# Transposing attention probabilities in 32x32 squares on VectorE and moving the squares by DMA and ScalarE, in place of TensorE transposes

## What is computed

```python
# x: (8, 1024, 384) float32, adj: (8, 1024, 1024) bool, six heads of 64 features
q = _heads(seq_inputs @ Wq + bq)
k = _heads(seq_inputs @ Wk + bk)
v = _heads(seq_inputs @ Wv + bv)
scores = jnp.einsum('bhqd,bhkd->bhqk', q, k) / np.sqrt(HEAD_SIZE)
bias = jnp.where(graph_mask, 0.0, NEG)[:, None]
probs = jax.nn.softmax(scores + bias, axis=-1)
ctx = jnp.einsum('bhqk,bhkd->bhqd', probs, v)
ctx = ctx.transpose(0, 2, 1, 3).reshape(seq_inputs.shape[0], seq_inputs.shape[1], H)
return ctx @ Wf + bf
# and around it
x = _layernorm(x + _L0_gnn_ref(x, ...), axis=-1)
```

## Time and profile before

| | before |
|---|---|
| time, median of three runs | 1510.48 us (1510.31 to 1511.2) |
| profiled execution, its time | 1509.4 us |
| its span | 1507.4 us |
| granted TensorE clock over the span | 0.997 of full speed |
| TensorE matmuls busy | 1471.1 us, 98% |
| VectorE busy | 898.2 us, 60% |
| ScalarE busy | 873.4 us, 58% |
| GpSimd busy | 378.2 us, 25% |
| DMA engines, share of their time on the kernel's own queue | 10.5% |

### The profile page before, as it was taken

The page is one execution under the profiler, slowest core; times in us unless marked ns, Lnnn a source line. Parts: engine busy times, 40 slices in busy tenths (PEclk is TensorE's granted clock), DMA queues, the critical chain, the costliest instruction groups (busy, mean ns, idle before and its releaser), DMA issues.

```text
span 1507.4 us, 32054 instructions
## 1 busy us (share of the span) xinstructions
PE 1471.1 (98%) x11088; PEld 1141.7 (76%) x11088; DVE 898.2 (60%) x1769; ACT 873.4 (58%) x1637; POOL 378.2 (25%) x676
## 2 busy tenths in 40 slices
PE   7999999999999999999999999999999999999996
PEld 6777787777877778777787777877778777787764
DVE  5666645665556655666555665566655666465654
ACT  4566626666266662666636665366654666546662
POOL 2112242122411224122141221412214122141222
PEclk9999999999999999999999999999999999999998
DMA  3110101100011000100001100011001110000000
GB/s 129 36 40 30 29 27 38 38 29 29 27 50 29 29 29 24 50 30 29 30 24 50 40 29 20 29 49 35 29 19 37 50 29 30 15 25 19 30 22 28
DMA packets 47925, 51.41 MB, mean 34 GB/s; under 512 B 9089, under 2 KB 47745, under 8 KB 47745
## 3 DMA queue, kind: packets, MB, share of 16 engines
q1 hardware_dynamic: 47744, 49.12, 10.5%
HBM read 36.31 MB, written 12.78 MB: 33 GB/s over the span
## 4 chain that ended last, share of the span: by engine, by line
PE 92%; DVE 3%; issue 2%; ACT 1%; POOL 1%; DMA 0%; DVEq 0%; SPq 0%; ACTq 0%; POOLq 0%
PE turn_ps L457 23%; PE context_ps L470 22%; PE score_ps L444 20%; PE misc_ps L356 4%; PE misc_ps L355 4%; PE misc_ps L354 4%; PE score_ps L354 3%; PE score_ps L355 3%; PE score_ps L356 3%; DVE prob L660 1%; PE context_ps L354 1%; PE turn_ps L354 1%; PE context_ps L356 1%; PE context_ps L355 1%; PE misc_ps L362 1%
## 5 line engine op out<-in xcount | busy, mean ns | idle before, releaser
L660 DVE CUSTOM_DVE_ANT_0 prob<-score_ps,mask 128x1024 f32<-128x1024 f32 x384 | 455.0, 1222 | 252.5 <-PE score_ps L444 232.7
L568 ACT ACTIVATE prob_t<-turn_ps 128x512 f32<-128x512 f32 x384 | 229.5, 598 | 431.6 <-PE turn_ps L457 431.6
L559 ACT ACTIVATE prob<-prob,row_min 128x1024 f32<-128x1024 f32 x384 | 442.1, 1151 | 64.3 <-DVE row_min L660 64.3
L457 PE MATMUL turn_ps<-ident,prob 128*128 128x128 f32 x3072 | 413.1, 276 | 9.8 <-ACT prob_t L568 5.5
L457 PEld LDWEIGHTS turn_ps<-ident,prob 128*128 128x128 f32 x3072 | 337.7, 140 | 94.8 <-issue 78.0
L470 PE MATMUL context_ps<-prob_t,v_all 128*64 128x256 f32 x3072 | 372.1, 385 | 0.8 <-ACT prob_t L568 0.8
L470 PEld LDWEIGHTS context_ps<-prob_t,v_all 128*64 128x64 f32 x3072 | 204.6, 136 | 148.9 <-issue 64.0
L806 POOL TENSOR_TENSOR context_lo<-context,context_hi 128x256 fp32r<-128x256 f32 x96 | 70.6, 735 | 938.6 <-ACT context_hi L582 938.6
L669 DVE COPY prob_t<-turn_ps 128x512 f32<-128x512 f32 x192 | 131.7, 686 | 30.7 <-PE turn_ps L457 30.2
L444 PE MATMUL score_ps<-k_hi,q_hi 64*128 64x512 f32 x768 | 140.9, 444 | 4.8 <-issue 3.8
L444 PE MATMUL score_ps<-k_lo,q_hi 64*128 64x512 f32 x768 | 120.4, 390 | 0.0
(11 more groups left out here) (85 smaller groups left out, 1834.9 us busy)
## 6 DMA issues: line engine op xcount, KB each, us to landing
x_in<-in_x_dram SPq DMA_DIRECT2D x32, 384.0 KB, 3.4
inv_rows<-spread_dram SPq DMA_DIRECT2D x192, 64.0 KB, 2.6
out_dram<-res SPq DMA_DIRECT2D x32, 384.0 KB, 2.5
adj_in<-in_adj_dram SPq DMA_DIRECT2D x64, 128.0 KB, 2.2
spread_dram<-inv_turned SPq DMA_DIRECT2D x384, 0.5 KB
prob_t<-in_L_gnn_Wk_dram SPq DMA_DIRECT2D x1, 576.0 KB, 4.3
prob_t<-in_L_gnn_Wq_dram SPq DMA_DIRECT2D x1, 576.0 KB, 7.1
prob_t<-in_L_gnn_Wv_dram SPq DMA_DIRECT2D x1, 576.0 KB, 8.3
```

The source lines that it names most:

```text
L457: last = pe.transpose(turn_ps[:, half, i, :], prob[:, u % 4, kt * P:(kt + 1) * P], ident[:])
L559: nc.scalar.activation(prob[:, t % 4, :], prob[:, t % 4, :], ACT.Exp, scale=-1.0, bias=row_min[:, t % 4:t % 4 + 1], accum_out=row_sum[:, t ...
L568: nc.scalar.activation(prob_t[:, pair % 2, head, 0:4, qt * P:(qt + 1) * P], turn_ps[:, 0], ACT.Copy).then_inc(copied[0], 1)
L660: nc.vector.tensor_tensor_reduce(prob[:, t % 4, :], score_ps[:, t % 2, :], mask[:, qt, :], 1.0, HUGE, ALU.add, ALU.min, row_min[:, t % 4:t ...
```

## The change

The change writes the kernel anew around another way to transpose the probabilities. Its parts:

1. `turn` and the copies out of `turn_ps` are gone. `turn_squares` on VectorE transposes `prob` (128x1024) in place, which turns each 32x32 square where it is. A square (a, c) that stands in partition block `a` belongs in block `c`. `move` on SyncE issues twelve DMAs for each slot, for all a other than c, each 32 partitions x 2 heads x 256 elements, and `move` on ScalarE copies the four pieces with a = c. The tokens of the keys are kept in another order in `xt_hi` and `xt_lo` (`tokens`), so that this gives the layout that `mix` reads.
2. `prob` is a ring of three slots (`RING = 3`). `mask_scores` of slot `s` waits until all 16 pieces of slot `s - 3` have landed. `mix` waits for the pieces of its two slots, and runs in one piece of 16 matmul pairs at slot 2g + 3 or later (the list `STEADY`).
3. `spread` and its DMAs are gone. GpSimd multiplies an identity matrix with the inverse sums (`make_diagonal`), and TensorE spreads them with two matmuls of 256 columns (job `i`, `spread_inverses`). ScalarE copies them to `context`.
4. Jobs go through three banks `job_ps`. ScalarE takes `v`, `i`, `k`, `q` and `x` jobs from PSUM; for `k`, `q` and `x` it writes both the high part and a full copy `raw`, from which GpSimd makes the low part. VectorE has none of these any more. The bias of `v` goes through the output bias instead.
5. Inputs are read twice (once for `x_in`, once for `res`), in DMAs of 128x384, and stores are of 128x384 as well. The first and the last batch are written out and the six between are a loop.
6. Projections for the next batch are spread over its predecessor's slots and its own first slots, and no `TAIL` stands between two batches. Before the first slot only `k` and `q` of the first head pair are made.

```diff
+    0: [("k", 2, 0, 0), ("k", 2, 1, 0), ("p", -4, 0, 0)],
+    1: [("q", 2, 0, 0), ("i", -1, 0, 0), ("m", -1, 0, 0)],
...
+    5: [("i", 0, 0, 0), ("m", 0, 0, 0), ("q", 1, 1, 0)],
+    6: [("i", 1, 0, 0), ("m", 1, 0, 0)],
+    7: [("i", 2, 0, 0), ("m", 2, 0, 0)],
+    8: [("q", 2, 1, 0), ("p", -2, 0, 0), ("p", -1, 0, 0)],
+    9: [("i", 3, 0, 0), ("m", 3, 0, 0)],
+    10: [("x", 0, 0, 1), ("x", 1, 0, 1), ("x", 2, 0, 1), ("q", 0, 2, 0), ("p", 0, 0, 0)],
+    11: [("i", 4, 0, 0), ("m", 4, 0, 0)],
...
+    20: [("k", 0, 0, 1), ("k", 0, 1, 1)],
...
+        def move_square(queue, s, a, c):
+            group, qt, ring = s // 2, s % 2, s % RING
+            queue.dma_start(prob_t[32 * c:32 * c + 32, group % 2, :, qt, a, :],
+                            prob[32 * a:32 * a + 32, 2 * ring:2 * ring + 2, GQ * c:GQ * c + GQ]
+                            ).then_inc(landed[ring], 16)
...
-            def spread(b, pair):
-                sp.wait_ge(inv_done, b * PAIRS + (pair + 1))
-                sp.wait_ge(context_done, b * PAIRS + (pair + 1))
-                for i in range(4):
-                    sp.dma_start(spread_dram[pair % 2, :, 32 * i:32 * i + 32],
-                                 inv_turned[32 * i:32 * i + 4, pair % 2, :]).then_inc(spread_out[pair % 2], 16)
-                sp.wait_ge(spread_out[pair % 2], b * (32 * PAIRS) + 64 * (pair // 2 + 1))
-                for head in range(2):
-                    src = spread_dram[pair % 2, 2 * head:2 * head + 2, :].rearrange("c p -> (c p)")
-                    sp.dma_start(inv_rows[64 * head:64 * head + 64, pair % 2, :],
-                                 src.partition_broadcast(64)).then_inc(spread_in[pair % 2], 16)
...
+            def move(b, s):
+                sp.wait_ge(squared, at(b, UNITS, 2 * s + 2))
+                if s % 2 == 0:
+                    sp.sem_inc(sp_waited, 1)
+                    sp.wait_ge(mixed, at(b, GROUPS, s // 2 + 1))
+                for a in range(4):
+                    for c in range(4):
+                        if not (a == c):
+                            move_square(sp, s, a, c)
...
-            def turn(b, u):
-                if u == 0:
-                    pe.wait_ge(job_out, jobs_through(b, EARLY_V[3], True))
-                pe.wait_ge(exp_done, b * UNITS + (u + 1))
-                for half in range(2):
-                    pe.wait_ge(copied[half], b * UNITS + (u + 1))
-                    for i in range(4):
-                        kt = 4 * half + i
-                        last = pe.transpose(turn_ps[:, half, i, :], prob[:, u % 4, kt * P:(kt + 1) * P], ident[:])
-                    last.then_inc(turned[half], 1)
...
-                for kt in range(4 * chunk, 4 * chunk + 4):
-                    for head in range(2):
-                        col = (2 * (pair % 3) + head) * HS
-                        last = pe.matmul(context_ps[64 * head:64 * head + 64, 0:GQ],
-                                         v_all[:, kt, col:col + HS], prob_t[:, pair % 2, head, kt, :],
-                                         start=(kt == 0), stop=(kt == TT - 1))
...
+            def spread_inverses(b, job):
+                pe.wait_ge(diag_done, at(b, GROUPS, job[1] + 3))
+                for head in range(2):
+                    last = pe.matmul(job_bank(b.mode, job)[64 * head:64 * head + 64, 0:GQ], ones[:],
+                                     diag[:, 2 * head:2 * head + 2, :], start=True, stop=True)
+                last.then_inc(job_done, 1)
...
+            def mix(b, group):
+                pe.wait_ge(context_done, at(b, GROUPS, group + 2))
+                for s in (2 * group, 2 * group + 1):
+                    pe.wait_ge(landed[s % RING], at(b, 256 * SLOTS // RING, 256 * (s // RING + 2)))
+                if group == 0:
+                    pe.wait_ge(job_out, out_through(b, ("v", TT - 1, 0, 0)))
+                for kt in range(TT):
+                    for head in range(2):
+                        col = (2 * (group % 3) + head) * HS
+                        keys = prob_t[:, group % 2, head, :, :, 32 * kt:32 * kt + 32].rearrange(
+                            "p q a j -> p (q a) j")
+                        last = pe.matmul(context_ps[64 * head:64 * head + 64, 0:GQ], v_all[:, kt, col:col + HS], keys,
+                                         start=(kt == 0), stop=(kt == TT - 1))
+                last.then_inc(mixed, 1)
...
-            def copy_first(b, u):
-                pair, head, qt = u // 4, u % 2, u % 4 // 2
-                if u % 4 == 0:
-                    act.wait_ge(mixed, b * PAIRS + (pair + 1))
-                act.wait_ge(turned[0], b * UNITS + (u + 1))
-                nc.scalar.activation(prob_t[:, pair % 2, head, 0:4, qt * P:(qt + 1) * P],
-                                     turn_ps[:, 0], ACT.Copy).then_inc(copied[0], 1)
...
+            def evict(b, job):
+                kind, n, _, _ = job
+                act.wait_ge(job_done, done_through(b, job))
+                bank = job_bank(b.mode, job)
+                if kind == "v":
+                    nc.scalar.activation(v_all[:, n, :], bank[:, 0:H], ACT.Copy).then_inc(job_out, 1)
+                    return
+                if kind == "i":
+                    act.wait_ge(context_lo_done, at(b, GROUPS, n + 1))
+                    nc.scalar.activation(context[:], bank[:, 0:GQ], ACT.Copy).then_inc(job_out, 1)
+                    return
+                at_split = SPLITS[b.mode].index(job)
+                copy = raw[:, raw_half(b.mode, job), :]
+                if kind == "x":
+                    half = slice(512 * job[2], 512 * job[2] + 512)
+                    nc.scalar.activation(tokens(xt_hi, n, half), as_tokens(bank), ACT.Copy).then_inc(hi_done, 1)
+                else:
+                    width, hi, _ = job_parts(job)
+                    which = 1 if kind == "k" else 0
+                    nc.scalar.activation(hi, bank[:, 0:width], ACT.Identity,
+                                         bias=bias_qk[:, which, n:n + 1]).then_inc(hi_done, 1)
+                reg, per, const = in_front(b, len(START_JOBS), SPLITS)
+                act.wait_ge(lo_done, reg * per + (const + at_split - 1))
+                if kind == "x":
+                    nc.scalar.activation(copy, bank, ACT.Copy).then_inc(job_out, 1)
+                else:
+                    nc.scalar.activation(copy[:, 0:width], bank[:, 0:width], ACT.Identity,
+                                         bias=bias_qk[:, which, n:n + 1]).then_inc(job_out, 1)
...
+            def move(b, s):
+                act.wait_ge(squared, at(b, UNITS, 2 * s + 2))
+                if s % 2 == 0:
+                    act.wait_ge(mixed, at(b, GROUPS, s // 2 + 1))
+                group, qt, ring = s // 2, s % 2, s % RING
+                for a in range(4):
+                    rows = slice(32 * a, 32 * a + 32)
+                    nc.scalar.activation(prob_t[rows, group % 2, :, qt, a, :],
+                                         prob[rows, 2 * ring:2 * ring + 2, GQ * a:GQ * a + GQ],
+                                         ACT.Copy).then_inc(landed[ring], 16)
...
-            def copy_even_second(b, u):
-                pair, head, qt = u // 4, u % 2, u % 4 // 2
-                if u % 4 == 0:
-                    dve.wait_ge(mixed, b * PAIRS + (pair + 1))
-                dve.wait_ge(turned[1], b * UNITS + (u + 5))
-                nc.vector.tensor_copy(prob_t[:, pair % 2, head, 4:8, qt * P:(qt + 1) * P],
-                                      turn_ps[:, 1]).then_inc(copied[1], 1)
-            def divide(b, pair):
-                dve.wait_ge(mixed, b * PAIRS + (pair + 3))
-                dve.wait_ge(spread_in[pair % 2], b * (16 * PAIRS) + 32 * (pair // 2 + 1))
-                dve.wait_ge(context_lo_done, b * PAIRS + (pair + 1))
-                nc.vector.tensor_tensor(context[:], context_ps[:, 0:GQ], inv_rows[:, pair % 2, :],
-                                        ALU.mult).then_inc(context_done, 1)
...
+            def turn_squares(b, t):
+                ring = 2 * (t // 2 % RING) + t % 2
+                dve.wait_ge(exp_done, at(b, UNITS, t + 1))
+                dve.sem_inc(dve_waited, 1)
+                nc.vector.transpose(prob[:, ring, :], prob[:, ring, :]).then_inc(squared, 1)
+            def invert_sums(b, group):
+                dve.wait_ge(exp_done, at(b, UNITS, 4 * group + 4))
+                dve.wait_ge(diag_done, at(b, GROUPS, group + 1))
+                nc.vector.reciprocal(inv_sum[:, group % 2, :], row_sum[:, group % 2, :]).then_inc(inverted, 1)
+            def divide(b, group):
+                dve.wait_ge(mixed, at(b, GROUPS, group + 3))
+                dve.wait_ge(job_out, out_through(b, ("i", group, 0, 0)))
+                nc.vector.tensor_tensor(context[:], context_ps[:, 0:GQ], context[:],
+                                        ALU.mult).then_inc(context_done, 1)
...
+            def low_part(b, job):
+                pool.wait_ge(job_out, out_through(b, job))
```

(9 more changed lines are left out.)

856 lines of the change are left out of this document (421 added, 435 removed), and 14 rows, old and new, of the table STEADY.

## The result

The changed kernel takes 1797.36 us (median of four runs, 1792.93 to 1799.17), against 1510.76 us (four runs) for the kernel before: a ratio of 1.1893, with a 95% interval of 1.1868 to 1.1917. It is slower by 19%, where the prediction said 1395 us with a range of 1305 to 1570. Its profiled execution has a span of 1791.0 us.

What follows compares the result with a forecast made beforehand. SyncE's DMA queue was taken as the bound: 2304 moves at 0.512 us, 1180 us, plus 213 us for other DMAs, waits and the ends, gave 1393 us, stated as 1395 us with a range of 1305 to 1570.

Steps and rivals of the forecast that it cites:

- SyncE as the bound: SyncE's in-order queue, issuing twelve moves a slot, sets the time at 1393 us, above the compute engines' 1308; chance 0.45.
- Its price: Issue of one move on SyncE: 0.512 us, taken from the opening loads, within 0.47 to 0.64.
- The term of 1180 us: SyncE's issue of all moves: 2304 at 0.512 us each.
- slower than I take it: Rival: moves issue on SyncE at line 310's rate, 0.64 us, giving 1688 us; chance 0.24 together with the clock.
- The DMA engines: Transfers of the moves: 768 packets a slot at 53 ns, 2.5 us of a 7.2 us slot, not a bound.
- Transposes and copies: Per slot, VectorE's transposes take 1.2 us each and ScalarE's four copies 2.1 us.
- the rival with 1.63: VectorE's transpose takes 1.63 us, not 1.2, bringing the compute engines to about 1391 to 1420 us; chance 0.08.
- The lockstep: TensorE and ScalarE tied slot by slot, the larger counting: about 1308 us; as rival bound 1308 to 1340, chance 0.23.
- The clock: Rival: TensorE's clock falls in idle time, time past 1500 us; given little, within 0.24 shared with slow SyncE issue.
- The ring doesn't bind: Three-slot ring of prob: reuse of a place needs 14 us against three slots of 7.2.
- What would show it: Signs if right: SyncE hardly waits, moves start 0.51 us apart, landings are awaited, slots even at 7.1, TensorE busy 85%.
- The skill's rule: DMA initiation is usually small beside the transfer, so SyncE would not be the bound and the compute engines' time would hold.

Runs made afterwards that it cites:

- tuned_back: Changed kernel with four moves on ScalarE's queue, late copies, slot 4's moves behind both exponentials of slot 5, diagonals early in slots 5 and 6; 1525.0 us.
- even_again: tuned_back with job i and mix one slot later, other jobs mostly in odd slots and three more piles undone; 1449.08 us (0.9594).
- six_dmas: Changed kernel issuing six of the twelve moves a slot, half of the squares left out but for the first four slots; 1513.85 us (1.0021).
- queues_only: Changed kernel with four of the twelve moves on ScalarE's queue, two behind each exponential of the next slot; 1545.72 us (1.0248).
- evict_spread: tuned_back with x and v jobs shared out over other slots; 1554.28 us (1.0290).
- pool_issues: Changed kernel with three of the twelve moves of a slot issued by GpSimd instead of SyncE; 1635.16 us (1.0822).

## Why the prediction was wrong

**SyncE as the bound: right. Its price: wrong, and this is the error.** "I take 0.512: the opening rows are plain copies to SBUF in runs, as the new ones are" failed. Those rows are plain loads from DRAM, and no row was a transfer from SBUF to SBUF. A move steps 0.639 (mean 0.665), where plain loads step 0.47. The row that I set aside had the price: the second broadcast of line 310 took 0.60 in the earlier trace rows, with its gap 0.64, and a move takes the same 0.597. The term of 1180 us measured 1538. The rival "slower than I take it" gave 1688 us at 0.64: the right price from the right row, but for a wrong reason, since it named 64 packets of 1 KB, and a move of 1 KB in all costs the same. I gave it, together with the clock, a chance of 0.24. The other 103 us are steps above 0.64 (63), other DMAs and waits (33) and the ends (6).

**The DMA engines: right.** 223488 packets took 43.5% of 16 x 1791 us, 56 ns each, for 53 predicted, and half the bytes gained 34 us.

**Transposes and copies.** 1.2 us was right (1231 ns, two in 2.38), and the rival with 1.63 falls. The copies take 627 ns, four in 2.58 us where I had 2.1: 0.5 us a slot, off the bound in the changed kernel.

**The lockstep: wrong by 205 us, hidden by the first error.** 1308 us was the sum of each slot's larger engine; with six moves it measured 1514. It left out the waits between the queues: a fourth job needs a bank, which ScalarE gives back only behind two exponentials, job `i` needs a diagonal that GpSimd makes late, and the next scores stand behind both. From tuned_back to even_again the lists change (and the place of one diagonal), and that is worth 76 us; late copies, on six_dmas, are worth 69. The rest, up to the 1308, stays open.

**The clock.** I gave it little, for "waits would be below 2 us each". One was 5.82 in six_dmas and the longest for landings 7.7 in the changed kernel, and its mean clock was 0.864 (0.997 before). TensorE's matmuls were busy for 1345.7 us instead of 1186; in even_again, at 0.94, 1235.7. It isn't the cause of 1797, since a move costs 0.597 on an idle chip too and SyncE hardly waits; in six_dmas, at 0.918, TensorE was busy for 1242.0 us. What the clock costs there was not separated.

**The ring doesn't bind**: masks waited 21.9 us for landings. **What would show it**: SyncE hardly waits and `mix` waits for landings, as written; the moves started 0.64 apart, not 0.51, TensorE was busy for 75%, not 85%, and slots went from 5.0 to 15.1 us (means over the six middle batches), 9.2 on average, not an even 7.1.

**The skill's rule.** The Trainium skill (DMA: Bandwidth & Descriptors, Issuing engines are not separate DMA queues) calls initiation "usually small relative to the DMA itself". One move does land 2.0 us after its issue, for 0.6 of issue, but landings overlap and issues don't, and 2304 issues took 1538 us of the 1791, so the trace doesn't agree. Perfetto Trace Analysis of the same Trainium skill (DMA Optimizations) says that sharing out DMAs over the engines that can issue them may help when the issuing engine is what looks busy; queues_only agrees, with 252 us.

## What to carry to other kernels

Before making one engine's work into many DMAs, multiply their number by the step of a run of the same kind of transfer, and measure that kind if no row has it: here 0.64 us for SBUF to SBUF on one queue, 7.7 us for twelve, from 1 KB to 64 KB alike. A second queue's issues can lie beside long instructions of its engine. Where engines share few buffers, don't add up maxima by slot: look for the job that needs a buffer whose release stands behind other work, and spread such jobs before shortening single waits, with an eye on who waits for each job in its new place (evict_spread lost 29 us).

## What the runs showed of the hardware

- In runs of one shape, the issue of a DMA from SBUF to SBUF took 0.59 to 0.62 us (medians) for 1 KB to 256 KB, a plain load from DRAM to SBUF 0.42 to 0.43, a copy from DRAM to DRAM 0.60. Four of 512 KB took 0.49, 0.60, 0.79 and 1.21. A move took 0.597 on an idle chip as in the kernel.
- A load right behind a move took 0.584 us to issue (3 of them), apart 0.346.
- SyncE's and ScalarE's queues issued at once at 0.64 and 0.67 us; GpSimd's took 0.53 a step (12 in 6.46 us), landing 15.6 us later beside large copies, 2.2 in pool_issues.
- TensorE had clock 0.50 for 3.8 us after an idle stretch of 5.82 us, and 1.00 in the 2.5 us behind that.
